# First mixture stage of a four-block network: the two gate broadcasts of a pair in two row tiles of TensorE

## The reference, cut to what matters

```python
def _L0_ffn_ref(x, gate_w, gate_b, W1, b1, W2, b2):
    logits = xf @ gate_w + gate_b                 # xf: 2048 tokens x 64
    probs = softmax(logits)
    top2_vals, top2_idx = top_k(probs, 2)
    cw = zeros((N, 8)).at[arange(N)[:, None], top2_idx].add(top2_vals)
    for each expert e:                            # 8 experts
        h = gelu(xf @ W1[e] + b1[e])              # 64 -> 128
        y = h @ W2[e] + b2[e]                     # 128 -> 64
        out += cw[:, e] * y
```

## Time and profile before

| | |
|---|---|
| Median of 3 runs | 633.27 us (632.72 to 633.65) |
| The profiled execution's own time | 630.24 us |
| Its span, first to last instruction | 628.4 us |
| TensorE busy | 517.3 us, 82% of the span |
| VectorE busy | 358.9 us, 57% |
| ScalarE busy | 283.9 us, 45% |
| GpSimd busy | 148.3 us, 24% |
| Mean granted TensorE clock | 0.947 of full |

### The profile page before, as it was taken

One profiled execution on the slowest core, in us unless ns is written; L12 is line 12 of the kernel. 1 busy time (PEld: TensorE's weight loads), 2 busy tenths in 40 slices (PEclk: granted clock), 3 DMA queues, 4 the chain that ended last, 5 costly groups with the idle time before them and its releaser, 6 DMA issues. The chain is left out here.

```text
span 628.4 us, 12008 instructions
## 1 busy us (share of the span) xinstructions
PE 517.3 (82%) x5122; PEld 282.6 (45%) x5122; DVE 358.9 (57%) x574; ACT 283.9 (45%) x392; POOL 148.3 (24%) x140
## 2 busy tenths in 40 slices
PE   2889989968997994777787888757997898699994
PEld 0463338834223784766766642323323234333231
DVE  1253895165556437977886456465336696722534
ACT  2452222335551218999899526443671102333330
POOL 9900000020002000897887600006003002000000
PEclk9899999998999996999999897876999999799998
DMA  7000000020000005554453000110002000000000
GB/s 272 1 3 2 2 1 2 0 96 3 0 1 30 2 6 206 197 189 158 169 197 109 2 18 1 49 39 0 0 2 108 1 0 0 2 0 1 0 18 17
DMA packets 7989, 29.90 MB, mean 48 GB/s; under 512 B 864, under 2 KB 2176, under 8 KB 7552
## 3 DMA queue, kind: packets, MB, share of 16 engines
q1 hardware_dynamic: 7936, 29.14, 13.4%
HBM read 28.47 MB, written 0.67 MB: 46 GB/s over the span
## 5 line engine op out<-in xcount | busy, mean ns | idle before, releaser
L1008 PE MATMUL PS<-GX,OH 128*128 128x64 f16 x2304 | 74.5, 196 | 25.7 <-DVE OH L1170 19.3
L1008 PEld LDWEIGHTS PS<-GX,OH 128*128 128x128 f16 x2304 | 72.0, 100 | 30.3 <-DVE OH L1170 15.3
L1095 ACT ACTIVATE DIST<-BC,wbuf 128x2048 f16<-128x2048 f16 x24 | 48.0, 2001 | 2.6 <-DMA BC<-idx_dram 0.8
L1897 DVE TENSOR_SCALAR HID<-PS,wbuf 128x512 f32<-128x512 f32 x32 | 23.8, 750 | 41.6 <-PE PS L1790 41.6
L1098 ACT ACTIVATE OH<-DIST 128x2048 f16<-128x2048 f16 x24 | 45.9, 1911 | 0.8
L1170 DVE TENSOR_SCALAR OH<-BC,wbuf 128x2048 f16<-128x2048 f16 x48 | 44.1, 942 | 2.3 <-DMA BC<-idx_dram 2.3
L943 POOL TENSOR_TENSOR V<-SQ 128x512 f32<-128x512 f32 x18 | 27.9, 1550 | 58.7 <-DVE SQ L1181 57.9
L144 PE MATMUL PS<-X,wconst 128*128 128x512 f32 x32 | 20.2, 765 | 24.0 <-DMA wconst<-pack_dram 9.7
L1786 PE MATMUL PS<-Y,wbuf 64*128 64x512 f32 x128 | 36.6, 615 | 2.3 <-DVE HID L1897 1.5
L1836 ACT ACTIVATE HID<-PS,wbuf 128x512 f32<-128x512 f32 x32 | 22.0, 687 | 36.4 <-PE PS L1790 36.4
L163 ACT ACTIVATE SQ<-PS 128x512 f32<-128x512 f32 x16 | 9.6, 597 | 63.2 <-PE PS L144 63.2
(11 more groups left out here) (301 smaller groups left out, 950.3 us busy)
## 6 DMA issues: line engine op xcount, KB each, us to landing
BC<-idx_dram SPq DMA_DIRECT2D x36, 512.0 KB, 4.0
wbuf<-pack_dram SPq DMA_DIRECT2D x1, 2082.5 KB, 11.7
wbuf<-pack_dram SPq DMA_DIRECT2D x1, 1656.0 KB, 7.0
wbuf<-pack_dram SPq DMA_DIRECT2D x1, 1494.5 KB, 6.3
wbuf<-pack_dram SPq DMA_DIRECT2D x1, 820.0 KB, 13.2
wconst<-pack_dram SPq DMA_DIRECT2D x1, 759.5 KB, 7.3
wbuf<-pack_dram SPq DMA_DIRECT2D x1, 732.0 KB, 4.1
wbuf<-pack_dram SPq DMA_DIRECT2D x1, 602.5 KB, 3.7
```

The lines of the kernel that those rows point to most:

```text
L1008: mm = pe.matmul(o, OH[:, s % NOH, qh, t * P:(t + 1) * P], src, start=(qh == 0 and part == 0), stop=(qh == 1 and part == 1))
L1095: after_act(act, act.activation(DIST[:, :], BC[:, s % NBC, :], ACT.Abs, bias=wt("negq1")))
L1897: dve.tensor_scalar(HID[:, n % 8, :], bank(2 + n % 4), wt("b1_3", 2 * e + m, 1), 0.0, ALU.add, ALU.max).then_inc(hid_in_v, 1)
```

## The change

The second half's gates are put at partitions 64 to 87 instead of in further columns of partitions 0 to 23, and the broadcast of a step with `bh` = 1 reads them there, in row tile 64. `CWT3` becomes half as wide. The transposes of the second eight token tiles go to output partitions 64 to 87, ScalarE's second copy moves those partitions, and the host packs `sel24` twice, in rows 0 to 23 and 64 to 87 (`twice`). The number, kind, shape and order of the instructions on every engine stay as they were, except that GpSimd clears half as many columns (L721).

```diff
-            CWT3 = sb("CWT3", [P, TILES * P], BF16, sctx)
+            CWT3 = sb("CWT3", [P, COLS], BF16, sctx)
...
-                    pe.matmul(bank(2 + n % 3), SELB[0:C, e * P:(e + 1) * P], CWT3[0:C, (2 * bh + bp) * HC:(2 * bh + bp + 1) * HC],
-                              start=True, stop=True, tile_position=(0, 0)).then_inc(bc_ps, 1)
+                    r = C * bh
+                    pe.matmul(bank(2 + n % 3), SELB[r:r + C, e * P:(e + 1) * P], CWT3[r:r + C, bp * HC:(bp + 1) * HC],
+                              start=True, stop=True, tile_position=(r, 0)).then_inc(bc_ps, 1)
...
-                        mm = pe.transpose(o[0:3 * E, i * P:(i + 1) * P], CW3[:, t, :, :].rearrange("p s e -> p (s e)"), IDB[:, :])
+                        mm = pe.transpose(o[C * q:C * q + 3 * E, i * P:(i + 1) * P], CW3[:, t, :, :].rearrange("p s e -> p (s e)"), IDB[:, :])
...
-                    act.activation(CWT3[0:3 * E, q * 1024:(q + 1) * 1024], bank(2 + q).bitcast(BF16)[0:3 * E, :], ACT.Copy).then_inc(cwt_in, 1)
+                    act.activation(CWT3[C * q:C * q + 3 * E, :], bank(2 + q).bitcast(BF16)[C * q:C * q + 3 * E, :], ACT.Copy).then_inc(cwt_in, 1)
...
-    put("sel24", np.tile(np.eye(E, dtype=f), (3, 1)))
+    twice("sel24", np.tile(np.eye(E, dtype=f), (3, 1)))
```

## The result

In the first comparison, ten runs each, the changed kernel takes 626.5 us (median; 624.7 to 629.37) and the kernel before 630.62 (627.67 to 633.65). The ratio is 0.9929, with a 95% interval of 0.9906 to 0.9953. Three further comparisons of the same two kernels gave 0.994, 0.9966 and 0.9961 (see the experiments). Over all comparisons the other 45 runs of the changed kernel have a mean of 627.69 us and the 104 of the kernel before one of 630.45: **2.8 us less**, give or take 0.7 (twice the standard error, from standard deviations of 2.02 and 2.14). With the run at 635.45 it is 2.6.

A forecast was written before the change was run, and what follows sets the result against it. TensorE, busy throughout the loop, was taken to set its pace. Ten full rounds at 0.21 us (2.1) plus 0.48 in the last rounds gave 2.6 us off 633.27, so 630.7 us, range 629.5 to 631.8.

The forecast's parts named there:

- The pair holds the array as long as one: Broadcast pair in the loop: second starts under 0.01 us behind the first, saving 0.21 us per round, 2.1 over ten.
- The start gives nothing: Before the first full round: saving 0, since the first down waits for VectorE's second product; bound 2 x 0.21.
- The last rounds give 0.48: Last rounds, without up: three steps take 4.14 us instead of 4.62, with down waiting for VectorE's products.
- VectorE and ScalarE do not take over in the full rounds: Full rounds: 0.78 us of slack before down for VectorE's products, 0.5 before up for ScalarE's GELU.
- The copies cost nothing, 0.015 either way: ScalarE's copies of the gates ahead of the broadcasts: second copy's 1.0 us unchanged, 0.015 us allowed either way.
- The clock in the loop: Granted TensorE clock in the loop: expected to stay at 1.00; a fall after 160 us would prove the prediction wrong.
- no later stage changes its length: Behind the block: stages keep their length while the block ends 2.6 us earlier.
- the level and its scatter: Whole kernel: 2.6 us subtracted from the three runs' median, 633.27, giving 630.7; runs taken to lie 0.5 either side.
- the late second load (1): Broadcast pair: second weight load starts only after the first matmul; 0.12 saved per pair, 631.8 us; chance 0.05.
- no overlap (2): Broadcast pair stays one behind the other, 633.3 us; chance 0.06 together with rival 3.
- VectorE's chain in the full rounds (3): VectorE's products decide the loop if 0.78 us longer; 633.3 us if 0.99 longer; chance 0.06 together with rival 2.
- the clock (4): Clock falls in the loop, 1.7 us per stretch: 632.4 with one, 635.8 with three; chance 0.04 with the like.

The follow-up runs named there:

- b1_one: Changed kernel with one extra 128x512 fp32 product on VectorE between the two of each pair; 633.44 us, a single time.
- e1_copyshift: Changed kernel, but second-half transposes go to partitions 0 to 23 and ScalarE's second copy reads these, writing 64 to 87; the two copies last 2.05 us.
- a3_rows128: Changed kernel's layout without row tiles: each broadcast runs over 128 rows with zero weights in the other half; 631.83 us, ratio 1.0027 to the kernel before.
- b2_two: Changed kernel with two extra VectorE products between the two of each pair; 639.68 us, a single time.

## Why the prediction was right or wrong, point by point

- **The pair holds the array as long as one** (0.21 saved per round): right. The pair's group lasts 0.38 us, and rounds went from 2.494 to (182.50 - 159.66) / 10 = 2.284, with the pair at 159.66 the first of the full rounds. The share of 1.54 of 2, which the prediction estimated from the Trainium skill ("TensorE: Matmul & The Clock Gate", Part 3: Packing small matmuls), would have left rounds of 2.34, which no trace shows. The instruction of the same shape elsewhere in the trace was the better guide.
- **The start gives nothing**: right. From the first broadcast to the first full round it takes 159.66 - 155.85 = 3.81 us and took 161.18 - 157.38 = 3.80 (the copies before it come below).
- **The last rounds give 0.48**: right, 182.50 to 186.65 is 4.15 us against 4.14 worked out and 4.62 before. VectorE's chain binds there: an extra product in b1_one lengthens two of these rounds, while the full ones stay.
- **VectorE and ScalarE do not take over in the full rounds**, with 0.78 us of room: right, by the runs with one and two extra products.
- **The copies cost nothing, 0.015 either way**: wrong by a small amount. The step named the copies' length and left out the seams between them, which the profile before showed: two copies of 1.01 us in 1.92. With other partitions written, both seams are 0.12 to 0.14 longer, 0.26 together. The block's net saving is thus 2.3 us, and 1.9 to 2.2 where the four traces are compared whole with the one before, in which the stretch ahead of the copies was shorter (0.84 us against 0.89 to 1.23); 2.6 was forecast. That the written partitions are enough to cause it is shown by e1_copyshift; why the engine does so is not.
- **The clock in the loop**: right, 1.00. The remark that no later stage changes its length was wrong of single executions: the part behind the block took 431.0 to 434.0 us in the four traces of the changed kernel.
- **The step that failed is the level and its scatter**: "The three runs' median is 633.27 ... I subtract the same 2.6 from it", with "the runs lie 0.5 us to either side" as its width. Those three agreed within 1 us and lay high: they are the first three of the ten in the comparison, whose median is 630.62. The 104 runs of the kernel before reach from 626.64 to 635.69 us with a standard deviation of 2.14, and their mean is 630.45. So of the 4.2 us between the forecast of 630.7 and the measured 626.5, 2.65 is the level (633.27 - 630.62) and 1.5 is the difference in that comparison, 4.1 us by the medians where 2.6 was forecast. The warning was there: the profiled execution stood 3.0 us below the median of the three, which I reported and did not use. Of the 4.1 us, 2.3 is the block. The rest came back in part in the second comparison (3.3 us by the medians), not in the third and fourth (1.1 and 2.6), and its cause stays open beyond scatter. That 2.6 from the right level, 627.85, comes so near the 627.69 measured over all is partly luck, since the block gave 2.3.
- **Rivals**: the late second load (1), no overlap (2) and VectorE's chain in the full rounds (3) are excluded by the round's timeline; the clock (4) by its windows.

## What to carry to other kernels

Here two bf16 products over 64 rows that stood one behind the other in one row tile came to cost the time of one when each got its own row tile and bank. To price such a step, look for an instruction of the same shape elsewhere in the trace. When data move to other partitions, count the seams between the copies that write them and not only the copies. And take the level from the scatter of executions, the profiled one among them: three runs that agree do not show it.

## What the runs showed of the hardware that I had not expected

- Successive ScalarE copies overlap by 0.09 us (start to start 0.92 for a length of 1.01) while they write from partition 0 on, and not at all (1.04) when the next writes from partition 64 on, or comes back from there, even when both read from partition 0 (e1_copyshift). Only these two ranges were tried.
- TensorE takes a product for one row tile ahead of one for the other that stands before it in the program: with the order `up`, broadcast, `up`, broadcast the second `up` starts 0.01 us after the first, both broadcasts 0.96 us after it, and rounds stay at 2.28 us.
- A change of tile shape goes with a seam of about 0.1 us, and the weight load is not taken early then: broadcasts over 128 rows start 1.06 us after the `up` products instead of 0.96, with their load at the same moment instead of 0.43 us ahead (a3_rows128). A weight load for the same shape is taken early even while `up` streams in the same row tile (before, 168.24 for the broadcast at 168.66).
- Four VectorE products of 128 x 512 fp32 that do not wait start 0.60 us apart in b2_two, though each lasts 0.68: what one more product costs there is the step and not its length.
- Copying 24 x 1024 bf16 elements out of PSUM takes 0.7 us on VectorE and 1.0 on ScalarE.
